# Feed-forward weights, bias rows and first norms prepared inside the second cross attention, with its turns written out on four engines

## The chip, the cores and the metric

The kernel runs on one core of a Trainium2 chip. The core has five instruction streams, and each works through its own in order: PE (TensorE, matrix products and transposes), DVE (VectorE), ACT (ScalarE, functions), POOL (GpSimd) and SP (SyncE, which here only starts DMA transfers). They meet at semaphores. The metric is the device time in microseconds (us).

## The reference

Two batches of 512 tokens of width 512 (x) pass through two layers of a gated cross attention and a gated feed-forward each. The change lies where the last two of these four parts meet:

```python
# second cross attention: 16 heads of 32, keys 1008 + 16 of ctx_1024, q and k normed by head
x = x + tanh(g_xattn[1]) * _L1_xattn_ref(_layernorm(x), ctx_1024, ...)
# second feed-forward
def _act_quant(x):
    scale = 127.0 / clip(max(abs(x), axis=-1, keepdims=True), EPS)
    return clip(round(x * scale), -128.0, 127.0) / scale
def _weight_quant(w):                       # one scale for the whole matrix
    scale = 1.0 / clip(mean(abs(w)), EPS)
    return clip(round(w * scale), -1.0, 1.0) / scale
def _bitlinear(x, w, b):
    return einsum('bsd,hd->bsh', _act_quant(x), _weight_quant(w)) + b
h = gelu(_bitlinear(x, w1, b1))             # w1: 2048 x 512
x = x + tanh(g_ffn[1]) * _bitlinear(h, w2, b2)   # w2: 512 x 2048
```

So both weight matrices (4 MB each in f32) need the mean of their magnitudes before any element can be rounded to -1, 0 or 1. They depend on no activation.

## The kernel before

**The second cross attention** (cross_attention_1). After a front part that makes the queries, the scores are worked off in 8 turns: 4 groups of 4 heads (g) times 2 batches (b). A turn has 16 slots (n): 4 heads by 4 tiles of 128 queries. In slot n

- PE makes the 128 x 1024 scores of n (L2646), transposes the probabilities of slot n-3 (L2607) and in odd slots multiplies transposed probabilities by values (L2624); in slots 5 to 8 it also projects the outputs of the turn before (L2636);
- DVE takes the maximum of the scores of n (L2536, L2537), inverts the sums of n-1 (L2521), makes the low part of the transposed probabilities of n-3 (L2529) and in slots 5 to 8 adds a projected tile to x (L2546);
- ACT copies the high part of n-3 (L2558) and takes the exponentials of n (L2572);
- POOL multiplies the probabilities of n-1 by the inverted sums (L2592), which PE transposes two slots later.

`turns` (L2504) writes the first and the last turn out and puts the six between them into a loop of three iterations of two turns, on PE, DVE, ACT and POOL. SP has a loop of its own over groups: after the last scores of a turn it loads queries and keys of the next group, then its values, and after the turn's x is done the next rows of the output weights (L2319). What follows the last turn (the part "after") has no scores: the last transposes, the last values, and four projections, one behind the other because each waits until DVE has emptied the same bank.

**The feed-forward** (bit_ffn) starts when x is complete (x2_done). Its first matrix is loaded during the attention (raw[0]), the second when x is complete. `sizes` on ACT sums the magnitudes of each with one instruction of 128 x 8192 (L2829); PE sums over partitions with a matrix of ones; DVE makes mean and inverse (L2740, L2742) and scales and rounds 8 chunks of 128 x 2048 with two instructions each (L2748, L2750), ACT makes the third step and the bf16 copy (L2836). Then PE turns both matrices, 16 groups of 8 transposes (L2912), through four banks that ACT (even groups) and DVE (odd groups) empty. Only then do the tiles start: for each of 8 tiles of 128 tokens a norm with rounding on DVE (`norm`), its rounding and transposing (`norm_round`, `norm_turn`, `norm_turned`), the hidden layer on PE (`hidden`), gelu on ACT, `hidden_scale` on DVE, `hidden_round` on ACT, `hidden_turn` and `output` on PE, `add_out` on DVE. The norms run AHEAD = 3 tiles in front.

## Time and profile before

| | us |
|---|---|
| time, median of 3 runs | 2809.32 (2807.34 to 2811.43) |
| the profiled execution, its time | 2806.77 |
| its span in the trace | 2804.9 |

| of the span | busy us | share |
|---|---|---|
| PE | 2392.8 | 85% |
| DVE | 1716.1 | 61% |
| ACT | 1485.5 | 53% |
| POOL | 1096.4 | 39% |

The profiled execution is 1.9 us longer than its span, and 2.6 us below the median of the three runs. The turns of the second cross attention begin at about 2202 us; x is complete at 2642.95; the span ends at 2804.9. Everything before 2202 is the same program in both kernels. Engine shares are means over parts that differ; the rows below are from single stretches. "issue" in a row means that the trace shows nothing that the engine waited for.

### The profile page before, as it was taken

How to read it: one execution, taken by the hardware profiler on the slowest of the kernel's cores; microseconds unless marked ns; L12 is line 12 of the kernel's file. 1: busy time of each engine (PE TensorE's matmuls, PEld its weight loads, DVE VectorE, ACT ScalarE, POOL GpSimd, SP SyncE). 2: the span in 40 equal slices, each digit the busy share in tenths (PEclk: the TensorE clock that was granted, in tenths of full speed). 3: DMA queues.
4: the chain of work that ended last, by engine and by line, in shares of the span. 5: the costliest groups of instructions: out<-in, count | busy, mean ns of one | idle time of the engine just before them, and what ended most of it. 6: DMA issues, size and time to landing. Idle time of an engine off the chain costs nothing. (4 is left out here: it accounts for less than half of the span.)

```text
span 2804.9 us, 46131 instructions
## 1 busy us (share of the span) xinstructions
PE 2392.8 (85%) x14822; PEld 1987.3 (71%) x14830; DVE 1716.1 (61%) x3849; ACT 1485.5 (53%) x3054; POOL 1096.4 (39%) x1553
## 2 busy tenths in 40 slices
PE   5999999999984899898998474999995688989558
PEld 3778878787874788888887353999994576767434
DVE  2555555555554666666666663566655587878576
ACT  3444444444443666656665453444442686777565
POOL 0222232322231444444444265777772654444200
PEclk9999999999997899999999796999997899999869
DMA  3000000000001000000000465677665433233100
GB/s 113 20 12 12 14 19 11 7 19 11 7 1 41 20 1 19 19 19 19 19 19 1 164 207 187 184 202 190 192 177 137 128 91 88 64 74 107 64 1 30
DMA packets 123517, 189.90 MB, mean 68 GB/s; under 512 B 18260, under 2 KB 66644, under 8 KB 121748
## 3 DMA queue, kind: packets, MB, share of 16 engines
q1 hardware_dynamic: 111272, 160.67, 18.9%
q0 software_dynamic: 10992, 25.96, 4.3%
q10 hardware_dynamic: 1152, 2.10, 0.3%
q8 instruction: 42, 0.69, 0.1%
q14 instruction: 59, 0.48, 0.1%
HBM read 142.55 MB, written 46.14 MB: 67 GB/s over the span
## 5 line engine op out<-in xcount | busy, mean ns | idle before, releaser
L435 ACT ACTIVATE x_p<-x_p,x_least 128x1024 f32<-128x1024 f32 x128 | 147.3, 1151 | 307.2 <-DVE x_least L391 307.1
L469 POOL TENSOR_TENSOR x_carry<-x_rtotal 128x1 f32<-128x1 f32 x128 | 24.7, 193 | 559.8 <-DVE x_rtotal L368 559.8
L375 DVE TENSOR_TENSOR x_pT<-pair,x_pT 128x512 fp32r<-128x512 f32 x256 | 164.2, 683 | 122.6 <-ACT x_pT L454 122.6
L2159 PE MATMUL pair<-m_h,e_w 128*128 128x320 f32 x1536 | 230.4, 311 | 1.1 <-DVE m_h L2074 1.1
L2159 PEld LDWEIGHTS pair<-m_h,e_w 128*128 128x128 f32 x1536 | 228.9, 189 | 2.7 <-issue 1.5
L537 PE MATMUL pair<-x_pT,x_v 128*128 128x256 f32 x1536 | 209.6, 293 | 9.2 <-DVE x_pT L375 9.2
L537 PEld LDWEIGHTS pair<-x_pT,x_v 128*128 128x128 f32 x1536 | 194.0, 194 | 26.3 <-issue 18.3
L993 ACT ACTIVATE s_p<-s_p,s_least 128x128 f32<-128x128 f32 (+3 forms) x256 | 143.7, 561 | 123.1 <-DVE s_least L903 123.0
L565 PE MATMUL pair<-x_kT,x_qT 128*128 128x512 f32 x768 | 206.9, 404 | 0.0
L2536 DVE TENSOR_REDUCE z_most<-pair 128x1 f32<-128x1008 f32 x128 | 153.8, 1202 | 82.4 <-PE pair L2646 50.0
L1131 PE MATMUL pair<-s_pT,s_v 128*128 128x256 f32 (+1 forms) x1152 | 158.4, 284 | 47.2 <-DVE s_pT L880 47.2
L1131 PEld LDWEIGHTS pair<-s_pT,s_v 128*128 128x128 f32 x1152 | 152.8, 195 | 59.9 <-issue 30.9
L2558 ACT ACTIVATE z_pT<-pair 128x512 fp32r<-128x512 f32 x256 | 141.7, 601 | 96.2 <-PE pair L2607 81.5
L2607 PE MATMUL pair<-ident,z_p 128*128 128x128 f32 x1024 | 144.8, 281 | 50.8 <-DVE z_pT L2529 49.6
L1053 POOL TENSOR_TENSOR s_carry<-s_rtotal 128x1 f32<-128x1 f32 x256 | 49.7, 194 | 346.6 <-DVE s_rtotal L874 346.3
L2572 ACT ACTIVATE z_p<-pair,z_most 128x1008 f32<-128x1008 f32 (+1 forms) x256 | 174.3, 696 | 14.4 <-DVE z_most L2537 14.4
L2607 PEld LDWEIGHTS pair<-ident,z_p 128*128 128x128 f32 x1024 | 117.4, 143 | 90.4 <-DVE z_pT L2529 62.1
L2592 POOL TENSOR_SCALAR z_p<-z_p,z_rtotal 128x1008 f32<-128x1008 f32 (+1 forms) x256 | 174.5, 694 | 0.0
L880 DVE TENSOR_TENSOR s_pT<-pair,s_pT 128x128 fp32r<-128x128 f32 (+3 forms) x256 | 124.5, 487 | 81.3 <-ACT s_pT L979 81.2
L2529 DVE TENSOR_TENSOR z_pT<-pair,z_pT 128x512 fp32r<-128x512 f32 x256 | 162.7, 676 | 4.6 <-ACT z_pT L2558 3.8
L1808 POOL TENSOR_TENSOR e_w<-e_raw,e_w 128x2048 fp32r<-128x2048 f32 x32 | 146.7, 4588 | 40.2 <-ACT e_w L1774 40.2
L454 ACT ACTIVATE x_pT<-pair 128x512 fp32r<-128x512 f32 x256 | 138.3, 594 | 45.1 <-PE pair L523 45.1
(345 smaller groups left out, 6102.2 us busy)
## 6 DMA issues: line engine op xcount, KB each, us to landing
e_raw<-in_L_ffn_w SPq DMA_DIRECT2D x48, 1024.0 KB, 5.7
z_v<-z_vst SPq DMA_DIRECT2D x16, 768.0 KB, 3.6
z_kS<-z_k SPq DMA_DIRECT2D x24, 512.0 KB, 9.9
z_vS<-z_v SPq DMA_DIRECT2D x8, 1536.0 KB, 7.0
f_raw<-in_L_ffn_w SPq DMA_DIRECT2D x2, 4096.0 KB, 13.4
z_qS<-z_q SPq DMA_DIRECT2D x24, 256.0 KB, 4.4
s_wraw<-in_L_ffn_wq SPq DMA_DIRECT2D x9, 512.0 KB, 4.4
x_wq<-in_L_xattn_Wq SPq DMA_DIRECT2D x8, 512.0 KB, 3.6
```

Source lines behind the costliest of these rows:

```text
L375: dve.tensor_tensor(pT[1][:, keys, q * P:(q + 1) * P], TR[j][:, :].rearrange("p (k n) -> p k n", n=P), pT[0][:, keys, q * P:(q + 1) * P].b ...
L435: act.activation(p[n][:, :], p[n][:, :], ACT.Exp, scale=-1.0, bias=least[:, n:n + 1], accum_out=total[:, n:n + 1]).then_inc(s_ex, 1)
L537: mm = pe.matmul(OB[:, cols], v[x0][b][:, k, :], pT[x1][:, k, cols], start=(half == 0 and n == 0 and k == 0), stop=(half == 1 and n == 2 a ...
L565: mm = pe.matmul(SC[n % 2][:, j * BANK:(j + 1) * BANK], qT[x0][b][n // QT][:, n % QT * P:(n % QT + 1) * P], kT[x1][b][:, j * BANK:(j + 1) ...
L1131: mm = pe.matmul(OB[:, cols], v[b][:, k, first:first + 2, :].rearrange("p k d -> p (k d)"), pT[x1][:, k, cols], start=(i % 2 == 0 and half ...
L1808: pool.tensor_tensor(dst[1][:, :, :], raw[parity][:, :, :], dst[0][:, :, :].bitcast(F32), ALU.subtract).then_inc(s_lo, 1)
L2159: mm = pe.matmul(GU[m % 2][:, j * BANK:j * BANK + CAP], w[x0][:, c, m * P:(m + 1) * P], XS[s][x1][:, c, :], start=(n == 0 and c == 0), sto ...
L2529: dve.tensor_tensor(pT[1][:, k, cols], TR[i][:, :].rearrange("p (k n) -> p k n", n=P), pT[0][:, k, cols].bitcast(F32), ALU.subtract).then_ ...
L2536: dve.tensor_reduce(most[:, w, 0:1], SC[n % 2][:, 0:MAIN], AX.X, ALU.max, negate=True)
L2572: act.activation(p[w][:, cols], SC[n % 2][:, cols], ACT.Exp, bias=most[:, w, k:k + 1], accum_out=total[:, w, k:k + 1]).then_inc(s_ex, 1)
L2592: pool.tensor_scalar(p[w][:, cols], p[w][:, cols], rtotal[:, w, k:k + 1], 1.0, ALU.mult, ALU.mult).then_inc(s_pn, 1)
L2607: mm = pe.transpose(TR[i][:, k * P:(k + 1) * P], p[n % RING][:, kk * P:(kk + 1) * P], ident[:, :])
```

## The change

Three things are done.

1. `every_turn` takes the place of `turns` on DVE, ACT and POOL, and SP's loop over groups becomes a Python loop: all 8 turns are written out on these four engines. PE keeps `turns`, that is, its loop.
2. The weights are made during the turns. A slot is now counted from 0 to 127 over all turns. SP loads both matrices in 8 chunks of 1 MB through two ring buffers, twice. In the first pass ACT sums the magnitudes of chunk i behind slot 4i+3 (`magnitudes`, slots 3 to 31). The sums go to DRAM and come back to every partition (`loads`, turn 2), and DVE adds them up ahead of slot 42 (`means`), in place of the ones matrix. In the second pass POOL rounds chunk i with three instructions, behind slots 48+8i+1, +3 and +5 (`weights`), and behind slots 113, 115 and 117 makes the bias rows and the bf16 identity.
3. The feed-forward is entered differently. Statistics of the first four tiles are taken by DVE ahead of slot 12 of the last turn, their square root by ACT and the norms 0 and 1 by DVE in the part "after". After x2_done PE turns only the 8 groups of the first matrix; those of the second are put between the first tiles' work, through two banks.

The diff, cut to its core:

```diff
@@ back_sync: the loop over groups written out, with the loads
             def back_sync(sp):
-                with sp.Fori(0, NG - 1) as j:
+                sp.wait_ge(s_pj, PJ0 + KVO + NT)
+                for j in range(NG - 1):
                     for b in range(B):
+                        ffn["loads"](sp, B * j + b)
                         sp.wait_ge(s_sc, SC0 + NU * (B * j + b + 1))
...
+                for h in range(B * (NG - 1), TURNS):
+                    ffn["loads"](sp, h)
@@ turns
+            def every_turn(engine, body):
+                for h in range(TURNS):
+                    body(h // B, h % B, "first" if h == 0 else "last" if h == TURNS - 1 else "")
                 body(NG, 0, "after")
@@ back_vector, in slot n of turn h
+                        if own and h * NU + n == MEAN_AT:
+                            ffn["means"](dve)
+                        if part == "last" and n == NU - 4:
+                            ffn["statistics"](dve, 0)
+                        if part == "after" and n == 4:
+                            ffn["first norms"](dve)
...
-                turns(dve, body)
+                every_turn(dve, body)
@@ back_scalar, behind the exponentials of slot n
+                        if own:
+                            ffn["magnitudes"](act, h * NU + n)
+                        if part == "after" and n == LAG:
+                            ffn["root"](act, 0)
@@ back_gpsimd, behind the slot's products
+                        ffn["weights"](pool, h * NU + n)
@@ bit_ffn
+            def loads(sp, turn):
+                if turn == 0:
+                    load(sp, 0)
+                    load(sp, 1)
+                    for i in range(2, 5):
+                        sp.wait_ge(s_red, i - 1)
+                        load(sp, i)
...
+                elif turn == 2:
+                    sp.wait_ge(s_red, CHUNKS)
+                    for w in range(2):
+                        sp.dma_start(sizes[w], size[:, w, :]).then_inc(s_sum, 16)
+                    load(sp, 1)
+                    sp.wait_ge(s_sum, 32)
+                    sp.dma_start(ring[0][:, 0:2 * P * CH], sizes.rearrange("w p k -> (w p k)").partition_broadcast(P)).then_inc(s_sum, 16)
+                    sp.wait_ge(s_mean, 2)
+                    load(sp, 0)
+                elif turn < 7:
+                    for i in {3: (2, 3), 4: (4,), 5: (5, 6), 6: (7,)}[turn]:
+                        sp.wait_ge(s_wq, i - 1)
+                        load(sp, i)
...
+            def means(dve):
+                dve.wait_ge(s_sum, 48)
+                for w in range(2):
+                    dve.tensor_reduce(total[:, w:w + 1], ring[0][:, w * P * CH:(w + 1) * P * CH], AX.X, ALU.add).then_inc(s_mean, 1)
...
+            def magnitudes(act, slot):
+                if slot < SIZED + 4 * CHUNKS and slot % 4 == 3:
+                    i = (slot - SIZED) // 4
+                    act.wait_ge(s_w[i % 2], 16 * (i // 2 + 1))
+                    act.activation(ring[i % 2][:, :], ring[i % 2][:, :], ACT.Abs,
+                                   accum_out=size[:, i // CH, i % CH:i % CH + 1]).then_inc(s_red, 1)
+            def weights(pool, slot):
+                if ROUNDED <= slot < ROUNDED + 8 * CHUNKS:
+                    i, part = (slot - ROUNDED) // 8, slot % 8
+                    w, r = i // CH, ring[i % 2][:, :]
+                    if part == 1:
+                        pool.wait_ge(s_w[i % 2], 16 * (CH + i // 2 + 1))
+                        pool.wait_ge(s_mean, 4)
+                        pool.tensor_scalar(r, r, winv[:, w:w + 1], 1.0, ALU.mult, ALU.min).then_inc(s_wr, 1)
+                    elif part == 3:
+                        pool.wait_ge(s_wr, 2 * i + 1)
+                        pool.tensor_scalar(r, r, -1.0, MAGIC, ALU.max, ALU.add).then_inc(s_wr, 1)
+                    elif part == 5:
...
+                        pool.tensor_scalar(dst, r, -MAGIC, 1.0, ALU.add, ALU.mult).then_inc(s_wq, 1)
...
-            def sizes(act):
-                act.wait_ge(*x2_done)
-                for w in range(2):
-                    act.wait_ge(s_w[w], 16)
-                    act.activation(wq[w][:, :, :], raw[w][:, :, :], ACT.Abs, accum_out=size[:, w:w + 1]).then_inc(s_size, 1)
@@ tensor(pe), after the turns
+                for g in range(GROUPS):
+                    weight_turn(g)
...
                 norm_turn(0)
-                hidden(0)
+                for g in range(GROUPS, GROUPS + 4):
+                    weight_turn(g)
+                    if g == GROUPS + 1:
+                        hidden(0)
                 norm_turn(1)
+                for g in range(GROUPS + 4, 2 * GROUPS):
+                    weight_turn(g)
                 hidden(1)
```

What stands where on three engines:

ACT in the first turn, slots 2 to 4, before (z_p are probabilities, z_pT their transposes):

```order
L2572 ACTIVATE z_p,z_total<-pair,z_most 128x1008
L2572 ACTIVATE z_p,z_total<-pair,z_most 128x16
L2558 ACTIVATE z_pT<-pair 128x4x128 x2
L2572 ACTIVATE z_p,z_total<-pair,z_most 128x1008
L2572 ACTIVATE z_p,z_total<-pair,z_most 128x16
L2558 ACTIVATE z_pT<-pair 128x4x128 x2
```

and in the changed kernel (f_ring is the ring buffer, f_size the sums):

```order
L2591 ACTIVATE z_p,z_total<-pair,z_most 128x1008
L2591 ACTIVATE z_p,z_total<-pair,z_most 128x16
L2577 ACTIVATE z_pT<-pair 128x4x128 x2
L2591 ACTIVATE z_p,z_total<-pair,z_most 128x1008
L2591 ACTIVATE z_p,z_total<-pair,z_most 128x16
L2803 ACTIVATE f_ring,f_size<-f_ring 128x2048
L2577 ACTIVATE z_pT<-pair 128x4x128 x2
```

The sum over chunk 0 stands between slot 3's exponentials and slot 4's copy, and so does each of the seven others.

DVE ahead of slot 42 in the changed kernel, from the end of slot 40 on; before, the three f_ rows weren't there:

```order
L2565 SCALAR_TENSOR_TENSOR x<-pair,tgate,x 128x512
L2555 TENSOR_REDUCE z_most<-pair 128x1
L2556 TENSOR_REDUCE z_most<-pair 128x1
L2534 RECIPROCAL z_rtotal<-z_total 128x2
L2542 TENSOR_TENSOR z_pT<-pair,z_pT 128x4x128 x2
L2792 TENSOR_REDUCE f_total<-f_ring 128x1 x2
L2794 TENSOR_SCALAR f_wmean<-f_total 128x2
L2796 RECIPROCAL f_winv<-f_wmean 128x2
L2555 TENSOR_REDUCE z_most<-pair 128x1
```

Between the tile added to x in slot 8 of turn 2 and the sums over f_ring there is one slot of DVE's work.

PE from the last projections to the first hidden layer, before (L2900 is the ones matrix, L2912 the weights' transposes, L2922 and L2924 a norm's, L2935 and L2937 the hidden layer):

```order
L2636 MATMUL pair<-z_wo,z_oT 128x512 x8
L2900 MATMUL pair<-f_size,f_ones 128x2
L2912 MATMUL pair<-f_identb,f_wq 128x128 x128
L2922 MATMUL pair<-ident,f_u 4x128
L2924 MATMUL pair<-f_identb,f_hq 128x128 x4
L2935 MATMUL pair<-f_brows,f_uT 128x512
```

and in the changed kernel (f_wq_last is a quarter of the second matrix):

```order
L2660 MATMUL pair<-z_wo,z_oT 128x512 x8
L3025 MATMUL pair<-f_identb,f_wq 128x128 x64
L3041 MATMUL pair<-ident,f_u 4x128
L3043 MATMUL pair<-f_identb,f_hq 128x128 x4
L3025 MATMUL pair<-f_identb,f_wq 128x128 x3
L3025 MATMUL pair<-f_identb,f_wq_last 128x128
```

The last two rows stand four times before the first hidden layer (L3054). So of 128 transposes 64 and two further groups of 8 stand ahead of it now; the other six groups stand between it and the second.

## Rows read from the trace of the kernel before

**Rows 1.** Windows of two turns each: us, busy by engine, PE clock, DMA share, GB/s

```profile
2252.90:2353.00 100.10, 91.42 (x611) 73.19 (x610) 86.23 (x169) 79.05 (x198) 48.99 (x97) 1.00 0.35 86
2353.00:2462.20 109.20, 92.69 (x611) 74.66 (x610) 86.33 (x168) 79.24 (x197) 48.92 (x97) 0.97 0.30 76
```

**Rows 2.** Timeline at a loop's end: start, us, engine, line, operation, [idle before <-releaser]

```profile
2352.98 0.63 PE L2646 MATMUL pair<-z_kS,z_qS 96*128 96x512 f32 x2
...
2361.47 1.21 DVE L2536 TENSOR_REDUCE z_most<-pair 128x1 f32<-128x1008 f32 x1 [8.48 <-issue]
```

**Rows 3.** DMA queues in the window 2353 to 2571: packets, MB, share

```profile
q8 instruction: 1, 0.02, 0.0%
```

**Rows 4.** Timeline of an undisturbed pair of slots

```profile
2230.47 0.63 PE L2646 MATMUL pair<-z_kS,z_qS 96*128 96x512 f32 x2
...
2231.14 1.21 DVE L2536 TENSOR_REDUCE z_most<-pair 128x1 f32<-128x1008 f32 x1 [0.66 <-PE pair L2646]
2231.58 1.08 ACT L2558 ACTIVATE z_pT<-pair 128x512 fp32r<-128x512 f32 x2 [0.86 <-PE pair L2607]
...
2233.23 1.16 PE L2607 MATMUL pair<-ident,z_p 128*128 128x128 f32 x8 [0.79 <-DVE z_pT L2529]
```

**Rows 5.** Timeline of the first turn, where slot 3's exponentials end

```profile
2219.20 1.30 SPq L2307 DMA_DIRECT2D z_qS<-z_q  x3
...
2220.44 1.09 ACT L2558 ACTIVATE z_pT<-pair 128x512 fp32r<-128x512 f32 x2
```

**Rows 6.** DMA issues of the span: KB each, us from issue to landing

```profile
e_raw<-in_L_ffn_w SPq DMA_DIRECT2D x48, 1024.0 KB, 5.7
...
z_tbo<-in_L_xattn_bo SPq DMA_DIRECT2D x1, 256.0 KB, 6.5
```

**Rows 7.** Instructions on the tile f_raw: ns min/median/max, first and last start

```profile
L2836 ACT ACTIVATE f_wq<-f_raw x8: 1892/1910/1912, 2668.9 to 2686.1; 128x2048 bf16<-128x2048 f32 x8
```

**Rows 8.** Timeline of the third turn (slots 8 to 11)

```profile
2333.18 0.75 DVE L2546 SCALAR_TENSOR_TENSOR x<-pair,tgate,x 128x512 f32<-128x512 f32 x1
...
2334.11 4.32 SPq L2319 DMA_DIRECT2D z_wo<-in_L_xattn_Wo  x8
...
2336.82 1.21 DVE L2536 TENSOR_REDUCE z_most<-pair 128x1 f32<-128x1008 f32 x1 [0.43 <-PE pair L2646]
...
2340.71 0.19 POOL L2590 TENSOR_TENSOR z_carry<-z_rtotal 128x1 f32<-128x1 f32 x1 [0.92 <-DVE z_rtotal L2521]
```

**Rows 9.** Instructions of POOL by form: busy us, mean ns, idle before

```profile
L1808 POOL TENSOR_TENSOR e_w<-e_raw,e_w 128x2048 fp32r<-128x2048 f32 x32 | 146.7, 4588 | 40.2 <-ACT e_w L1774 40.2
...
L2592 POOL TENSOR_SCALAR z_p<-z_p,z_rtotal 128x1008 f32<-128x1008 f32 x128 | 142.1, 1110 | 0.0
```

**Rows 10.** Instructions on the tile stats: ns min/median/max, first and last start

```profile
L91 DVE BATCH_NORM_STATS2 stats<-x x24: 675/676/695, 9.1 to 2647.2; 128x6 f32<-128x512 f32 x24
```

**Rows 11.** Timeline from the last projections into the feed-forward

```profile
2633.72 0.75 DVE L2546 SCALAR_TENSOR_TENSOR x<-pair,tgate,x 128x512 f32<-128x512 f32 x1 [4.87 <-PE pair L2636]
...
2642.20 0.75 DVE L2546 SCALAR_TENSOR_TENSOR x<-pair,tgate,x 128x512 f32<-128x512 f32 x1 [2.08 <-PE pair L2636]
...
2697.82 0.54 DVE L2781 TENSOR_SCALAR f_h<-x,mv,rstd 128x512 f32<-128x512 f32 x1
...
2700.86 0.54 DVE L2781 TENSOR_SCALAR f_h<-x,mv,rstd 128x512 f32<-128x512 f32 x1
...
2703.38 0.79 PE L2935 MATMUL pair<-f_brows,f_uT 4*128 4x512 f32 x1 [0.83 <-ACT f_hqT L2857]
...
2714.83 0.18 PEld L2935 LDWEIGHTS pair<-f_brows,f_uT 4*128 4x128 f32 x1 [3.50 <-issue]
...
2724.75 2.29 DVE L2769 TENSOR_REDUCE f_most<-f_z 128x1 f32<-128x2048 f32 x1 [1.53 <-ACT f_z L2863]
```

**Rows 12.** Instructions of ACT from 2643 to 2725 by line: busy us, mean ns

```profile
L2822 ACT ACTIVATE f_w1T<-pair 128x1024 bf16<-128x1024 bf16 x4 | 4.0, 1016 | 1.0 <-PE pair L2912 1.0
...
L2849 ACT ACTIVATE f_hq<-f_h 128x512 bf16<-128x512 f32 x3 | 1.9, 630 | 3.9 <-DVE f_h L2786 3.9
```

More of the change, by code:

```diff
@@ L2695, in bit_ffn @@
             uT = [sb(f"f_uT{s}", [4, P], F32R) for s in range(2)]
-            with ExitStack() as early:
-                braw = early.enter_context(nc.sbuf_tensor("f_braw", [2, HID], F32))
-                blow = early.enter_context(nc.sbuf_tensor("f_blow", [2, HID], F32R))
-            z = [sb(f"f_z{s}", [P, HID]) for s in range(2)]
             zq = [sb(f"f_zq{s}", [P, HID], BF16) for s in range(2)]
@@ L2707, in bit_ffn @@
             TRZ = [banks[6 + i][:, :].bitcast(BF16) for i in range(2)]
-            WTB = [pairs[2 + i // 2][:, (i % 2) * BANK:(i % 2 + 1) * BANK].bitcast(BF16) for i in range(4)]
+            WTB = [banks[k][:, :].bitcast(BF16) for k in (6, 7, 4, 5)]
             s_w = [sem("f_w1"), sem("f_w2")]
-            s_b, s_size, s_sum, s_mean, s_wr, s_wq, s_wt, s_wa, s_wd = [
-                sem(f"f_{n}") for n in ("b", "size", "sum", "mean", "wr", "wq", "wt", "wa", "wd")]
+            s_b, s_red, s_sum, s_mean, s_wr, s_wq, s_wt, s_wa, s_wd = [
+                sem(f"f_{n}") for n in ("b", "red", "sum", "mean", "wr", "wq", "wt", "wa", "wd")]
@@ new lines, in half_statistics, with half_root @@
+            def half_statistics(dve, k):
+                tiles = range(k * QT, (k + 1) * QT)
+                dve.wait_ge(*(half_done, x2_done)[k])
+                for t in tiles:
+                    dve.bn_stats(stats[:, 6 * t:6 * t + 6], x3[:, t, :]).then_inc(s_stat, 1)
+                for t in tiles:
+                    dve.wait_ge(s_stat, 3 * NT + t + 1)
+                    dve.bn_aggr(mv[:, 2 * t:2 * t + 2], stats[:, 6 * t:6 * t + 6]).then_inc(s_mv, 1)
+            def half_root(act, k):
+                act.wait_ge(s_mv, 3 * NT + (k + 1) * QT)
+                act.activation(std[:, k * QT:(k + 1) * QT], mv[:, :].rearrange("p (t k) -> p t k", k=2)[:, k * QT:(k + 1) * QT, 1], ACT.Sqrt,
+                               bias=eps[:, 0:1]).then_inc(s_std, 1)
@@ L2721, in sync, with half_inverse @@
+            def half_inverse(dve, k):
+                dve.wait_ge(s_std, 4 + k + 1)
+                dve.reciprocal(rstd[:, k * QT:(k + 1) * QT], std[:, k * QT:(k + 1) * QT]).then_inc(s_rstd, 1)
+                dve.wait_ge(s_rstd, 4 + k + 1)
+            ffn["loads"], ffn["means"], ffn["weights"] = loads, means, weights
+            ffn["magnitudes"] = magnitudes
+            ffn["statistics"], ffn["root"] = half_statistics, half_root
             def sync(sp):
-                sp.wait_ge(*x1_read)
@@ L2754, in vector, with first_norms @@
+            def first_norms(dve):
+                half_inverse(dve, 0)
+                for t in range(2):
+                    norm(dve, t)
+            ffn["first norms"] = first_norms
+            def vector(dve):
+                for g in range(1, GROUPS, 2):
                     dve.wait_ge(s_wt, g + 1)
                     turned(dve, g)
-                dve.wait_ge(s_rstd, 5)
-                steps = 0
-                def step(ins):
-                    nonlocal steps
-                    steps += 1
-                    ins.then_inc(s_ch, 1)
-                    dve.wait_ge(s_ch, steps)
@@ L2881, in scalar @@
                 norm_round(0)
+                norm_round(1)
+                half_root(act, 1)
                 norm_turned(0)
-                norm_round(1)
-                norm_turned(1)
-                gelu(0)
+                for g in range(GROUPS, 2 * GROUPS, 2):
+                    act.wait_ge(s_wt, g + 1)
+                    turned(act, g)
+                    if g == GROUPS + 2:
+                        norm_turned(1)
+                        gelu(0)
                 norm_round(2)
@@ L2974, in tensor @@
                         norm_turn(t + AHEAD)
-            programs["ACT"].append(sizes)
-            statistics(3, x2_done, 1)
             programs["SP"].append(sync)
```

197 lines of the change are left out of this document (112 added, 85 removed).

## The prediction

> **What bounds the kernel now.** I read the stages first, then the chain, then the single waits. The stages: two turns without a loop's end take 100.1 us, the same 611 matrix instructions with one take 109.2 [rows 1], and the second such window, 2462 to 2571, repeats that. At the loop's end PE has already begun the next turn's scores at 2352.98, DVE comes back at 2361.47 after 8.48 us of "issue", that is, with nothing to wait for [rows 2]. Inside a turn PE and DVE hold each other: scores, DVE's maximum, DVE's low part, PE's transposes, values, and back; DVE idles 0.66 us and ACT 0.86 us in a pair of slots of 5.6 us [rows 4]. (In 100.1 us DVE is busy 86.2 and ACT 79.1 [rows 1]; most of the idle time lies in the slots with projections.) So whatever is put on DVE or ACT in an ordinary slot must fit into less than 1 us. After the turns, x is complete at 2642.20 + 0.75 = 2642.95 (T below), the first norm starts at 2697.82, the first hidden layer at 2703.38, the second at 2714.83 and DVE meets the second gelu at 2724.75 [rows 11]. From there on one tile follows the other at an even pace that the change leaves alone. Hence T to T+81.8 is the stretch to recompute.
>
> **What goes: the feed-forward's entry.** In the changed order, counted from T: PE's first 8 transposes about 0.5; ACT empties four banks at 1.02 [rows 12], T+4.5, while DVE empties the odd four. ACT then rounds two norms at 0.63 [rows 12], T+5.8. DVE takes statistics of the other four tiles, 4 x 0.68 [rows 10] with a little for the means, T+7.1; ACT's square root waits for that, and then come the small evictions (0.83 us of PE's waiting before [rows 11]): first hidden layer at T+8.4, where it was at T+60.4. It takes 7.8 us, as before in my reading of the trace from 2703.38 on; two groups of w2 and a norm's transposes bring PE to about T+17.7. ACT: eviction of that norm, table load and gelu to T+22.0, one eviction of w2 to T+23.0, and only then can PE fill that bank again and finish w2: second hidden layer at T+24.0 instead of T+71.9 [rows 11]. What follows is as before. **Gain 48 us.** The first layer alone would say 52; the interleaved w2 groups give 4 back, since the bank is waited for behind gelu. With all of PE's pieces at the half clock it is 45.
>
> **What goes: the loop's ends.** Two of them at 109.2 - 100.1 = 9.1 [rows 1], **18.2 us**; a third pass ends by falling through and shows no gap. What is late next is PE's own loop, which stays. Between 2353 and 2571, two further passes, the instruction queue 8 moves one packet [rows 3], and PE's scores at 2352.98 came without a gap, so PE has its loop at hand and I count its branch at nothing. The Trainium skill, "Runtime: NRT & Kernel Launch", section on instruction fetch mechanics, says that prefetch is purely sequential and a taken branch to a target outside the current two pages forces a fetch; it also gives PE four times the buffer. DVE's 8.48 us agree with the first half; taken to the letter for PE too, the rule would leave the stall where it is and make this term 0. The queue's row speaks for 18.2.
>
> **What comes: ACT's eight sums.** One is 1.91 us for 2048 columns [rows 7] with 0.19 to read the sum, 2.1. It stands ahead of the copy of the next slot. ACT idles 0.86 there, DVE may start 0.3 after the copy's first half, so some 1.0 is exposed; seven times, one of them in a projection slot where PE is behind anyway: **6 us** (0 to 14).
>
> **The first sum waits for its data.** SP's last loads for the front start at 2219.20 and take 1.3 to issue, and only behind them comes chunk 0, about 2220.7. ACT is through with slot 3 and goes on with the next copy at 2220.44 [rows 5], where it now waits. A 1 MB load lands 5.7 after its issue [rows 6]; here 768 KB go ahead of it and a second chunk beside it, so I take 7.5. With the sum itself and some slow clock after the pause, **10 us** (6 to 14). Behind the waiting ACT are the copies that DVE and then PE need, so all stand.
>
> **DVE ahead of slot 42 waits for the sums' round trip.** SP can only send them after its eight loads of output weights, which start at 2334.11 when x's last tile of the turn before is done and take 3.75 to 4.3 [rows 8]. Then two stores and chunk 1 (1.2), the stores' landing (about 1.9, from my reading of the 64 KB loads), and the broadcast of 512 KB behind 1 MB of chunk 1. The nearest row is the last of three loads, 1.5 MB in all, that lands 6.5 after its own issue [rows 6]. Issue at about 2341, landing at about 2347. DVE would begin slot 42 at 2336.82 [rows 8]: 10 us of waiting, then two sums over 512 (some 0.7 each) and two small operations, 1.9; with PE's clock down for a while after such a pause **13 us** (8 to 18). Behind DVE's wait the maximum of slot 42 is queued, for which ACT and PE wait.
>
> **POOL's 24 roundings.** A tensor_scalar of 1008 columns takes 1.11 [rows 9], so 2048 take about 2.0 to 2.2 (the dearest two-tensor form 4.59 [rows 9], which bounds it above; I take the nearer form). Eight slots cost POOL 12.4, three roundings 6.3, of 22.4: it fits, and a result is used two slots later. Two places don't fit. Chunk 7 is issued behind the output weights of turn 6, so it lands about 2334.1 + 3.8 + 0.4 + 5.7 = 2344 on turn 2's scale, while POOL is through with its slot at about 2339.8 and has the next one due at 2340.71 [rows 8]; with the rounding this makes that slot 5.5 late, of which some 2.2 are slack: **3 us**. The bias row's difference in slot 115 (4.6 by the two-tensor row, on two partitions) **1 us**.
>
> **DVE's early statistics and norms.** Four statistics in slot 12 of the last turn: 2.8, less DVE's idle 0.66: **2.3 us**. Norms 0 and 1 cost 2700.86 - 2697.82 = 3.04 each, 6.3 with the inverse; DVE idled 4.87 before the first projection [rows 11], and ACT's table load and root hold the norms back by 0.8: **2.3 us**.
>
> **Sum.** 48 + 18.2 = 66.2 off; 6 + 10 + 13 + 3 + 1 + 2.3 + 2.3 = 37.6 on; net 28.6. The profiled execution took 2806.8, so 2778.2; it stood 2.6 below the median of the runs, and on the median's scale it is 2780.7. I say 2780.
>
> **The rivals.**
> - *The two waits are short.* Speaks for it: the DMA engines are idle from 2224 on, and a lone 1 MB load is quick; against it: SP's order, which fixes the issue. With both at half my price it is 2780 - 10 = 2770; with ACT's sums hidden as well, 2765.
> - *The fetch stall stays*, at PE's branch, or because straight code on DVE and ACT runs into the 12 MB of further loads in the turns. For it: the rule above, and that both ends of loop fell into a burst of loads; against it: [rows 3], and turns 0 and 7, straight code under loads, show no gap. 2780 + 18 = 2798.
> - *Everything added is exposed*: ACT's sums at 2.1, POOL's roundings pushing one slot in each chunk by 1. 2780 + 8 + 8 = 2796.
> - *Slower than before: POOL's roundings run at the two-tensor rate.* One mechanism: two slots with a rounding need 3.1 + 4.6 = 7.7 against 5.6. In each chunk the first rounding then costs 1.1 (4.6 less 1.3 of gap, less 2.2 of slack), the next two 2.1 each; 5.3 a chunk, 42 in all: 2780 + 42 = 2822. It decides from about 4.1 us for one rounding. For it: all rows of two-tensor form on POOL; against it: 128 rows of the very form at 1.11.
>
> **How the numbers follow.** Forecast 0.56 (2770 to 2790), short waits 0.14, stall stays 0.11, all exposed 0.12, POOL slow 0.05, and 0.02 for nothing of this. 0.2% (about 5.6 us) is what a measurement can tell from no change. The range 2764 to 2799 takes in the first four. Faster takes all four cases but their edges, 0.91; slower is POOL's case and a rest, 0.05; same 0.04.
>
> **What would show it.** In the profile after: no 8 us of "issue" on DVE and ACT in the turns, and two turns without additions at 100.1; a wait of ACT of some 7 us for f_ring in the first turn, and one of DVE of some 10 in the third; POOL's roundings near 2.1; one wait of POOL for chunk 7 in the seventh turn; the first hidden layer 8 to 9 us and the second about 24 us after x is complete. The prediction is wrong if a gap of 8 us appears on PE at its branch, if a rounding takes over 3 us, or if the entry gives less than 45.

## The result, and the profile after

The changed kernel takes **2843.35 us** (median of 4 runs, 2838.82 to 2848.59) against 2809.26 for the kernel before in the same comparison: ratio 1.012, 95% interval 1.0108 to 1.0132. It is 34 us slower; 2780 had been forecast. The profiled execution took 2838.82, its span is 2837.0. Each experiment below was measured beside the kernel before in a comparison of its own, in which that kernel's median lies between 2809 and 2817 us; between comparisons the ratios count, not the medians.

The table cuts the spans at the same instructions: the front's last load of queries (where the row of turn 0 begins), then the first load of queries after each turn's last scores, and the end of x's last tile (T). "No clamp" is the first experiment below. In the forecast the 6 us of ACT's seven other sums are spread evenly, three to turn 0 and four to turn 1.

| stretch, us | before | after | no clamp | forecast for after |
|---|---|---|---|---|
| turn 0 | 30.2 | 42.7 | 43.8 | 42.8 |
| turn 1 | 50.2 | 54.3 | 52.6 | 53.6 |
| turn 2 | 49.9 | 63.9 | 65.7 | 62.9 |
| turns 3 and 4 | 109.2 | 126.5 | 100.2 | 100.1 |
| turn 5 | 59.2 | 64.7 | 50.1 | 50.1 |
| turns 6, 7 and the rest, to T | 125.0 | 151.7 | 135.6 | 133.6 |
| T to the end | 162.0 | 114.1 | 115.6 | 114.0 |
| together | 585.7 | 618.0 | 563.5 | 557.1 |

The feed-forward's entry gave what was forecast. The timeline of the kernel after, from x's last tile (which ends at T = 2722.92) to DVE's meeting with the second gelu (start, duration, engine, line, instruction, idle time before it and what ended it), answers to [rows 11]:

```profile
2722.17 0.75 DVE L2565 SCALAR_TENSOR_TENSOR x<-pair,tgate,x 128x512 f32<-128x512 f32 x1 [2.08 <-PE pair L2660]
...
2731.20 0.50 PE L3054 MATMUL pair<-f_brows,f_uT 4*128 4x512 f32 x1 [1.68 <-ACT f_hqT L2969]
...
2746.77 0.79 PE L3054 MATMUL pair<-f_brows,f_uT 4*128 4x512 f32 x1
...
2756.81 2.29 DVE L2877 TENSOR_REDUCE f_most<-f_z 128x1 f32<-128x2048 f32 x1 [1.64 <-ACT f_z L2975]
```

First hidden layer 8.3 us behind T (forecast 8.4), second 23.9 (24.0), DVE at the second gelu 33.9 where it was 81.8: 47.9 gained of 48.

The time went in the turns from slot 48 on, where POOL rounds. POOL's three roundings of each chunk, by form (busy us, mean ns), stand against [rows 9]:

```profile
L2814 POOL TENSOR_SCALAR f_ring<-f_ring,f_winv 128x2048 f32<-128x2048 f32 x8 | 57.3, 7166 | 2.9 <-DMA f_ring<-in_L_ffn_w 2.9
...
L2817 POOL TENSOR_SCALAR f_ring<-f_ring 128x2048 f32<-128x2048 f32 x8 | 56.7, 7091 | 0.0
...
L2823 POOL TENSOR_SCALAR f_wq<-f_ring 128x2048 bf16<-128x2048 f32 x7 | 13.3, 1899 | 0.0
```

Two of three take 7.1 us, 3.5 ns a column, where the 1.11 us of [rows 9] for 1008 columns had let 2.0 to 2.2 be expected. What that does to the others, in the timeline of the fourth turn:

```profile
2391.52 1.36 POOL L2615 TENSOR_SCALAR z_p<-z_p,z_rtotal 128x1008 f32<-128x1008 f32 x2
...
2392.86 7.16 POOL L2814 TENSOR_SCALAR f_ring<-f_ring,f_winv 128x2048 f32<-128x2048 f32 x1
...
2400.17 1.35 POOL L2615 TENSOR_SCALAR z_p<-z_p,z_rtotal 128x1008 f32<-128x1008 f32 x2
...
2401.65 1.97 PE L2631 MATMUL pair<-ident,z_p 128*128 128x128 f32 x8 [4.84 <-POOL z_p L2615]
...
2402.99 7.09 POOL L2817 TENSOR_SCALAR f_ring<-f_ring 128x2048 f32<-128x2048 f32 x1
```

POOL does its own products of slot 49 (z_p), then the 7.16 us, and only then the products of slot 50, for which PE has been waiting 4.84 us. Those of slot 51 and the second long instruction follow. Behind the wait PE's eight transposes take 1.97 us; those of an ordinary slot take 1.04 to 1.25 in this trace, so the pause costs clock as well. PE's wait stands in the list of waits (us in total, times, longest), together with the three that the change was expected to bring:

```profile
PE pair L2631 <- POOL z_p L2615: 53.8, 12, 7.7
...
DVE f_total L2792 <- DMA f_ring<-f_sizes: 10.4, 1, 10.4
...
ACT f_ring L2803 <- DMA f_ring<-in_L_ffn_w: 7.2, 1, 7.2
...
POOL f_ring L2814 <- DMA f_ring<-in_L_ffn_w: 2.9, 1, 2.9
```

Before, PE waited 1.1 us for z_p over the same stretch. The two turns that answer to the undisturbed pair of [rows 1], with POOL busy 108 us instead of 49 and PE's granted clock at 0.89 (columns as there):

```profile
2380.01:2506.52 126.51, 99.37 (x608) 80.64 (x608) 86.75 (x170) 79.80 (x197) 108.13 (x104) 0.89 0.33 91
```

### The profile page after: what moved, and what is told of

The parts are those of the page before. It is cut to its first block and busy times, and to the rows that moved or that the text cites. A ratio compares the mean times of both kernels' runs of the same rounds, so it can differ in the third digit from the quotient of the medians.

```text
span 2837.0 us, 45204 instructions
## 1 busy us (share of the span) xinstructions
PE 2411.6 (85%) x14828; PEld 2002.3 (71%) x14828; DVE 1698.1 (60%) x3834; ACT 1470.8 (52%) x3057; POOL 1230.3 (43%) x1580
## 5 line engine op out<-in xcount | busy, mean ns | idle before, releaser
L2631 PE MATMUL pair<-ident,z_p 128*128 128x128 f32 x1024 | 152.2, 293 | 107.6 <-POOL z_p L2615 54.8
L2631 PEld LDWEIGHTS pair<-ident,z_p 128*128 128x128 f32 x1024 | 125.2, 150 | 145.1 <-issue 82.2
```

What stands on the lines that cost most here:

```text
L2631: mm = pe.transpose(TR[i][:, k * P:(k + 1) * P], p[n % RING][:, kk * P:(kk + 1) * P], ident[:, :])
```

## The experiments

### What the roundings cost, and why

**The clamps left out (e1).** The two long instructions keep shape, types, place and waits; only an operation of each is another.

```diff
-pool.tensor_scalar(r, r, winv[:, w:w + 1], 1.0, ALU.mult, ALU.min)
+pool.tensor_scalar(r, r, winv[:, w:w + 1], 1.0, ALU.mult, ALU.mult)
-pool.tensor_scalar(r, r, -1.0, MAGIC, ALU.max, ALU.add)
+pool.tensor_scalar(r, r, 1.0, MAGIC, ALU.mult, ALU.add)
```

> The changed kernel with POOL's two clamps left out: (multiply, min 1) becomes (multiply, multiply by 1), and (max -1, add) becomes (multiply by 1, add); shapes, types, waits and number of instructions stay, and the weights' codes are no longer limited to -1..1. Theory A, the arithmetic function decides: both forms fall from 7.1 us to about 1.9, PE's waits for POOL's z_p fall from 54 us to under 5, x is complete some 60 us earlier, and the kernel takes 2775 to 2790. Theory B, a 2048-column f32 result written over its own source is slow on POOL, or DVE's and the loads' traffic slows it: both forms stay at 7.1 us and the time at 2839 to 2848. Theory C, POOL's instructions matter but another of the added waits takes their place: the forms fall to 1.9, and the time stays above 2800.

Measured: 2784.83 us (2784.14 to 2787.61), ratio to before 0.9902 (0.9886 to 0.9919). POOL by form:

```profile
L2814 POOL TENSOR_SCALAR f_ring<-f_ring,f_winv 128x2048 f32<-128x2048 f32 x8 | 16.0, 1999 | 2.8 <-DMA f_ring<-in_L_ffn_w 2.8
L2817 POOL TENSOR_SCALAR f_ring<-f_ring 128x2048 f32<-128x2048 f32 x8 | 15.3, 1910 | 0.0
```

Theory A holds; B and C are out. From turn 3 to T the run is 57.1 us shorter than the changed kernel (285.9 against 342.9), and turns 3 and 4 now take, in the window that answers to [rows 1], as long as the pair without a loop's end (100.15 and 100.10 us):

```profile
2384.39:2484.54 100.15, 91.43 (x608) 73.25 (x608) 86.19 (x170) 79.04 (x197) 69.69 (x107) 1.00 0.43 116
```

Of the 57.1 us, 43.0 are more idle time of PE. The other 14.1 are PE's same instructions taking longer (264.5 us busy against 250.4), at a granted clock of 0.88 to 0.93 in the rows from turn 3 to T, against 0.96 to 1.00 here.

**One clamp left out at a time (e2, e3).** The first pair of lines of this diff alone, and the second alone.

> The changed kernel with only (multiply, min 1) replaced by (multiply, multiply by 1); (max -1, add) stays (the codes have no upper limit). Theory A: the first form falls to 1.9 us and the second stays at 7.1; each of the 16 long instructions costs about as much of the end as another, so half of the loss comes back: 2805 to 2815. Theory B: nothing changes, 2839 to 2848. If one long instruction in a chunk fits into POOL's slack, nearly all comes back: below 2795.

> The changed kernel with only (max -1, add) replaced by (multiply by 1, add); (multiply, min 1) stays (the codes have no lower limit). Theory A: the second form falls to 1.9 us, the first stays at 7.1, 2805 to 2815, as with the other half left out. Theory B: 2839 to 2848. If only min were slow and not max: the second form at 7.1 with this edit would fall by nothing, and the run without min would have given all.

Measured: without (multiply, min) 2817.8 us, ratio 1.0023 (1.0013 to 1.0032); without (max, add) 2831.5, ratio 1.0068 (1.0052 to 1.0085). B is out again: the form whose clamp is left out falls to 2.0 and 1.9 us and the other stays at 7.1 and 7.2. But both times miss A's 2805 to 2815, and with them its even split: the first instruction of a chunk alone costs 43 us from turn 3 to T (328.9 against 285.9), the second alone 31. The timelines of PE show why. With only the first one long (e3), PE waits 4.83 to 4.85 us in each of the first seven chunks, and 8.13 us in the last:

```profile
2402.52 1.96 PE L2631 MATMUL pair<-ident,z_p 128*128 128x128 f32 x8 [4.85 <-POOL z_p L2615]
```

With only the second one long (e2), it waits 4.74 us in every other chunk and 0.8 to 0.9 in the ones between (the last chunk, whose data come late, has 2.5 and 3.7). In the ones between POOL's long instruction (2398.76 to 2405.86 in the first of them) falls into the slots with projections, and PE has two of them (L2660) to do meanwhile:

```profile
2399.30 1.98 PE L2660 MATMUL pair<-z_wo,z_oT 128*128 128x512 f32 x4 [0.22 <-ACT z_oT L2582]
...
2404.35 1.88 PE L2660 MATMUL pair<-z_wo,z_oT 128*128 128x512 f32 x4
...
2407.50 1.09 PE L2631 MATMUL pair<-ident,z_p 128*128 128x128 f32 x8 [0.81 <-POOL z_p L2615]
...
2436.11 1.96 PE L2631 MATMUL pair<-ident,z_p 128*128 128x128 f32 x8 [4.74 <-POOL z_p L2615]
```

That the projections are what fills the wait is read from this timeline; no run moved them. The waits of e3 add up to 7 x 4.84 + 8.13 = 42 us, but that they nearly equal its 43 is chance: PE's idle time grew by 34 us, and 9 are its slower instructions. Together the two long instructions cost 57, less than the sum of 74: behind the first one's wait the second finds PE later than it would otherwise, and in the changed kernel its waits of 4.74 are 2.6 to 3.0, those of 0.8 are gone, and only in chunk 7 it is 3.9.

**POOL's instructions alone (e0).** The changed kernel, and behind its end:

```diff
...
+                pool.wait_ge(s_x2, NT)
...
+                done(pool.memset(r1, 0.3))          # done: and wait for it
...
+                for _ in range(2):
+                    done(pool.tensor_scalar(r0, r1, one, 1.0, ALU.mult, ALU.min))
...
+                    done(pool.tensor_scalar(r0, r1, 1.0, -1.0, ALU.min, ALU.max))
...
```

> The changed kernel, and behind its last result 26 instructions of POOL alone, one after the other, with DVE, ACT, PE and the DMA queues idle (its total time is of no interest). Theory A, the function decides: over 2048 f32 columns every form with min or max takes about 7.1 us, also with another tile as target, with one operation only, and with a bf16 result; multiply with multiply, and multiply with add, take 1.9; time goes with the columns (1024: 3.6, 256: 0.9). Theory B, company on the memory's ports: alone, the forms with min or max take 1.9 to 4 as the others do. Theory C, two clamps in one instruction (min, max) cost twice one. Open, and of use for a repair: whether a comparison (is_gt) costs as little as a multiplication.

The timeline; in order (multiply, min), (multiply, multiply), (max, add), (multiply, add), min, max, (min, max), (multiply, is_gt); then (multiply, min) into bf16 and, last, a product of two tensors (left out: (multiply, min) 3.71 over 1024 columns and 1.14 over 256, a copy 1.89):

```profile
2844.58 7.16 POOL L3118 TENSOR_SCALAR f_ring<-f_ring,f_winv 128x2048 f32<-128x2048 f32 x1
2851.84 1.98 POOL L3119 TENSOR_SCALAR f_ring<-f_ring,f_winv 128x2048 f32<-128x2048 f32 x1
2853.90 7.09 POOL L3120 TENSOR_SCALAR f_ring<-f_ring 128x2048 f32<-128x2048 f32 x1
2861.08 1.90 POOL L3121 TENSOR_SCALAR f_ring<-f_ring 128x2048 f32<-128x2048 f32 x1
2863.06 5.37 POOL L3122 TENSOR_SCALAR f_ring<-f_ring 128x2048 f32<-128x2048 f32 x1
2868.51 5.36 POOL L3123 TENSOR_SCALAR f_ring<-f_ring 128x2048 f32<-128x2048 f32 x1
2873.95 1.89 POOL L3124 TENSOR_SCALAR f_ring<-f_ring 128x2048 f32<-128x2048 f32 x1
2875.95 7.17 POOL L3125 TENSOR_SCALAR f_ring<-f_ring,f_winv 128x2048 f32<-128x2048 f32 x1
...
2888.24 7.15 POOL L3128 TENSOR_SCALAR f_wq<-f_ring,f_winv 128x2048 bf16<-128x2048 f32 x1
...
2897.43 4.49 POOL L3130 TENSOR_TENSOR f_ring<-f_ring 128x2048 f32<-128x2048 f32 x1
```

B is out: alone, over a constant 0.3 and into another tile, the forms take the same 7.1 as among the turns. But A as I had put it is wrong as well, and so is C. (min, max) takes **1.89 us**, less than either alone (5.37). So it is not the function but the pair.

**More pairs, and DVE (e4).** The same frame with other pairs, and four of them on DVE behind POOL's.

> As the first run of instructions of POOL alone behind the changed kernel's end, with 15 other pairs of operations on 2048 f32 columns, and four of them on DVE. Theory P, a pair runs fast only if both operations are of one family (multiply, add, subtract, or min, max): (max, min), (min, min) and the two with a scalar in memory 1.9 us; (multiply, max), (add, min), (max, multiply), (min, multiply) 7.1. Theory Q, only the order (arithmetic first, then compare, or the other way) decides: one of the mixed orders at 1.9. One operation alone with no second: multiply and add at 1.9 if the missing second counts as nothing, at 5.4 as min and max alone did if the missing second is what is slow. On DVE all four forms take 1.2 to 2.3 us, the pairing plays no part.

(multiply, max); multiply alone; (add, add); (min, min); (max, min); (subtract, multiply); (min, max) with the first scalar from memory; then on DVE two instructions at a time, of which the first two are (multiply, min) and (multiply, multiply):

```profile
2849.64 7.16 POOL L3118 TENSOR_SCALAR f_ring<-f_ring,f_winv 128x2048 f32<-128x2048 f32 x1
2856.89 5.45 POOL L3119 TENSOR_SCALAR f_ring<-f_ring,f_winv 128x2048 f32<-128x2048 f32 x1
...
2869.60 7.11 POOL L3121 TENSOR_SCALAR f_ring<-f_ring 128x2048 f32<-128x2048 f32 x1
...
2883.96 7.08 POOL L3123 TENSOR_SCALAR f_ring<-f_ring 128x2048 f32<-128x2048 f32 x1
2891.12 7.08 POOL L3124 TENSOR_SCALAR f_ring<-f_ring 128x2048 f32<-128x2048 f32 x1
...
2918.07 7.10 POOL L3128 TENSOR_SCALAR f_ring<-f_ring 128x2048 f32<-128x2048 f32 x1
...
2937.89 1.97 POOL L3131 TENSOR_SCALAR f_ring<-f_ring,f_winv 128x2048 f32<-128x2048 f32 x1
...
2941.01 2.61 DVE L3140 TENSOR_SCALAR f_ring<-f_ring,f_winv 128x2048 f32<-128x2048 f32 x2 [95.25 <-POOL f_ring L3132]
```

Theories P and Q both fall. Of all the pairs tried four run at 0.93 to 0.97 ns a column: (multiply, multiply), (multiply, add), (min, max) and, in the kernels' third rounding, (add, multiply). The twelve others, (add, add), (subtract, multiply), (max, min) and (min, min) as well as every mixed one, take 3.5 ns; one operation with no second takes 2.6, even a multiplication, though a copy takes 0.92. What sets the four apart the traces do not show; they show only the times. On DVE the pairing plays no part: the first two instructions take 2.61 us together, (max, add) and (min, max) together 2.49, and each of the four 1.2 to 1.3. The Trainium skill, "GPSIMD Engine Reference", section 4.1 Engine selection, calls work with one input on this engine roughly line-rate. Of 16 pairs and 5 single operations here only the four pairs come near one column a nanosecond, and so does the copy (1.89 us). The Trainium skill, "GPSIMD Engine Reference", section 3.1, gives 4497 ns for a two-tensor addition of this size, and the product in the last row of the first list agrees with 4.49 us.

**The same three steps, paired for speed (f1).** Rounding comes before clamping, so that the clamp is a (min, max) against the constant plus and minus 1; the codes are complete.

```diff
-pool.tensor_scalar(r, r, winv[:, w:w + 1], 1.0, ALU.mult, ALU.min)
+pool.tensor_scalar(r, r, winv[:, w:w + 1], MAGIC, ALU.mult, ALU.add)
-pool.tensor_scalar(r, r, -1.0, MAGIC, ALU.max, ALU.add)
+pool.tensor_scalar(r, r, MAGIC + 1.0, MAGIC - 1.0, ALU.min, ALU.max)
```

> The changed kernel with the same three instructions a chunk on POOL, paired differently: (multiply by 1/mean, add the rounding constant), then (min, max) against the constant plus and minus 1, then as before; the clamp is complete. The instructions alone took 1.9 us for (multiply, add) and for (min, max), against 7.1 for (multiply, min) and (max, add). If the pairing is what decides: all three at 1.9 to 2.0 us among the turns too, and the time of the run without clamps, 2783 to 2788. If min and max are slow only with the other engines at work: the second stays above 5 us and the time is 2810 to 2820, as in the run with one long instruction a chunk.

Measured: 2787.9 us (2787.2 to 2795.1), ratio 0.9910 (0.9896 to 0.9925), that of the run without clamps within the intervals. The first instruction takes 1.99 us, and the (min, max) among the turns what it took alone:

```profile
L2817 POOL TENSOR_SCALAR f_ring<-f_ring 128x2048 f32<-128x2048 f32 x8 | 15.2, 1897 | 0.7
```

Two lines turn 1.2% slower into 0.9% faster.

### The loop's ends

The kernel before, with `every_turn` on DVE, ACT and POOL and nothing else (u1).

```diff
-                turns(dve, body)
+                every_turn(dve, body)      # and so on ACT and POOL
```

> The kernel before with one part of the change alone: the turns written out on DVE, ACT and POOL (SP and PE keep their loops, and the feed-forward is as before). My reading: the two gaps of 8 us of issue at the loop's ends go, turns 3 and 5 fall from 59.2 us to 50, and the time is 18.2 lower, 2791 to 2794. Rival, the fetch stall stays on PE's branch or comes back as gaps in straight code: the time stays within 5 us of before, and the gaps stand on PE or are scattered. Rival, SP's or PE's own loop was half of it: 9 lower, 2802.

Measured: 2795.7 us against 2815.75 in the same comparison, ratio 0.9927 (0.9914 to 0.9939): 20 us less, 18.2 forecast. Inside the traces, from the front's last load of queries to T, it is 405.7 us against 423.8, 18.1 less. SP's loads behind each turn's last scores:

```profile
2356.24 1.33 SPq L2307 DMA_DIRECT2D z_qS<-z_q  x3
...
2406.37 1.29 SPq L2307 DMA_DIRECT2D z_qS<-z_q  x3
...
2456.30 1.32 SPq L2307 DMA_DIRECT2D z_qS<-z_q  x3
```

These turns are 50 us apart, as are the others; the rivals are out. PE keeps its loop, and no gap stands at its branch. In the window 2353 to 2571 the queue "q14 instruction" moved 21 packets in the kernel before and moves 8 in this run, so the gaps went together with packets of instructions. The queue q8, from which the prediction took that PE has its loop at hand, moves one packet in both; which engine a queue serves the profile does not say.

### The two waits

**ACT's sums three slots later (f2).** On f1:

```diff
-            SIZED, ROUNDED = 0, 48
+            SIZED, ROUNDED = 3, 48
-                if slot < SIZED + 4 * CHUNKS and slot % 4 == 3:
+                if SIZED <= slot < SIZED + 4 * CHUNKS and (slot - SIZED) % 4 == 3:
```

> The run before this one, and ACT's eight sums each three slots later (slots 6, 10 to 34 in place of 3, 7 to 31). In the profile ACT waited 8.4 us for the first chunk; three slots are 8.4 us. My theory: that wait goes with some slow clock behind it, 8 to 11 us less, 2773 to 2778. Rival, the pause moves: chunk 0's landing is not what is late, or the last sum, now at slot 34, holds the sending of the sums and lengthens DVE's wait at slot 42 by as much: no gain, 2784 to 2788.

**The sums sent ahead of the output weights (f3).** On f1:

```diff
+                    if j == 0:
+                        ffn["sent"](sp)      # stores, load(1), broadcast: was in loads, turn 2
                     sp.wait_ge(s_wd, WD0 + QT * (B * j + B))
                     load_out(sp, j + 1)
```

> The run f1, and SP sends the sums (two stores, chunk 1's load, the broadcast) ahead of the eight loads of output weights instead of behind them; ACT's sums stay where they were. DVE waited 11.6 us for the broadcast at slot 42. My theory: the sums are there by slot 36, the wait goes with the slow clock behind it, 11 to 15 us less, 2770 to 2775. Rival, the output weights come later and PE's projections wait for them: half or none of it, 2778 to 2786.

In the run f1 that both start from, the waits are:

```profile
DVE f_total L2792 <- DMA f_ring<-f_sizes: 10.4, 1, 10.4
...
ACT f_ring L2803 <- DMA f_ring<-in_L_ffn_w: 7.9, 1, 7.9
```

Later sums: 2779.7 us, ratio 0.9868 (0.9853 to 0.9882) against 0.9910, 12 us by the ratios and 8 by the medians; ACT's wait is gone from the list, DVE's is 11.3. The wait goes, as my theory has it, but the time stays 2 us above its range: turns 0 and 1 take 10.9 us less, and turn 2, which begins earlier and still waits for the sums, 2.6 more (66.4 against 63.8). Sent early: DVE's wait is gone, turn 2 takes 53.2 us instead of 63.8, but the median is 2786.4 (2768.8 to 2791.2), ratio 0.9883 (0.986 to 0.9907), and my range of 2770 to 2775 is missed. The rival's reason is not it: no wait of PE for the output weights stands in the list. The profile has 10.7 us more behind turn 5 than f1 (258.2 against 247.5), with DVE's, ACT's and POOL's busy time the same and PE's 11.0 us longer for the same work; its granted clock is lower. Half of it lies in the last three projections, which take 3.78 us each here and 1.98 each in f1, behind gaps of the same length (3.04, 0.84 and 0.84). One execution of six kept the gain, and no profile of it was taken.

**All together (f4)**, with chunk 7's load ahead of the output weights as well:

```diff
+                    elif j == 2:
+                        ffn["seventh"](sp)   # wait_ge(s_wq, 6), load(7): was in loads, turn 6
```

> The run f1 (clamps paired as min with max) with both edits tried singly (ACT's sums three slots later, the sums sent ahead of the output weights) and a third: the load of chunk 7 ahead of the output weights of its turn, for which POOL waited 2.8 us. If each wait goes and none takes its place, the end of the turns comes 8 + 11 + 3 = 22 us earlier than in f1, and the time is 2762 to 2768. In f3 the turns were 11 us shorter and the whole only 2 in its profile (in one execution 19), because TensorE ran at half clock in more of the stretch from the last projections into the feed-forward (granted clock 0.70 and 0.76 there against 0.89 and 0.70). If that clock falls by chance from one execution to the next, the times here spread over some 15 us, 2762 to 2780; if an early end of the turns itself brings it, all executions stand near 2775.

Measured: 2765.8 us (2760.1 to 2771.0), ratio 0.9836 (0.9821 to 0.9852). It lies in the range of the first statement, and none of the three waits stands in the list any more. The spread of 11 us, with no execution near 2775, speaks for chance and not for an early end.

### The clock at the entry

The timeline of PE in f4: the second and third projection of the last turn, then the start of the first hidden layer.

```profile
2637.60 3.38 PE L2664 MATMUL pair<-z_wo,z_oT 128*128 128x512 f32 x4 [3.11 <-DVE x L2569]
2641.83 1.98 PE L2664 MATMUL pair<-z_wo,z_oT 128*128 128x512 f32 x4 [0.84 <-DVE x L2569]
...
2655.72 0.50 PE L3064 MATMUL pair<-f_brows,f_uT 4*128 4x512 f32 x1 [1.68 <-ACT f_hqT L2979]
2656.15 1.04 PE L3066 MATMUL pair<-f_w1T,f_hqT 128*128 128x512 bf16 x4
...
2657.54 1.89 PE L3066 MATMUL pair<-f_w1T,f_hqT 128*128 128x512 bf16 x4
```

The same projection takes 3.38 us and then 1.98, and in the hidden layer the same four products 1.04 and, 1.4 us later, 1.89: TensorE falls to 1.2 GHz behind a gap of 3.11 us, and behind gaps of 1.34 and 1.68 that follow each other, and comes back to 2.4. It is not so each time: in f1 the projection behind a gap of 3.04 takes 1.98, in f3 3.78. The granted clock of the stretch behind f4's last projection:

```profile
2647.00:2690.00 43.00, 33.06 (x221) 17.08 (x222) 25.40 (x57) 23.94 (x30) 0.00 (x0) 0.84 0.02 7
```

**The gaps filled with idle transposes (f5)**, up to T; on f4, with 6 more behind the last projection:

```diff
+                            if part == "after":
+                                fill(pe, 20 if t == 1 else 6)   # transposes of ident into TR[0]
                             pe.wait_ge(s_wd, WD0 + QT * (h - 1) + t)
```

> The run before this one, and 44 idle transposes of the identity on PE (results unused) in the gaps in which PE waits for DVE to add a tile of x: 20 before the second of the last four projections, 6 before the third and fourth, 6 before the weights' transposes. At full clock they fit into the gaps (0.84 to 3.04 us) to within 0.3 each. My theory: PE's pauses there are what lets the clock fall to its lower level, where a projection takes 3.8 us instead of 2.0 and the first hidden layer 9 instead of 5; with the pauses filled the clock stays at 1.00 to the end of the first hidden layer, and the time is 5 to 12 below the run before, and spreads less. Rival: the clock falls for another reason, the fillers only delay: 0 to 5 slower.

(The kernel has 38 of them, 20 + 6 + 6 + 6, and the trace shows as many; the 44 is a slip.) Measured: 2761.5 us (2755.2 to 2768.9), ratio 0.9816 (0.9802 to 0.9829). All four projections take 1.98, but the hidden layer is still at 1.89; the profile is that of the slowest execution. The intervals of f4 and f5 overlap: the gain of 4 us is not shown, and the executions spread by 14 us, not less than f4's 11.

**And on behind T (f6)**, 61 more, on f5:

```diff
+                idle(9)                      # transposes of ident into the output's bank
                 norm_turn(0)
...
+                        idle(11)
                         hidden(0)
...
+                    if g == 2 * GROUPS - 2:
+                        idle(28)
                     weight_turn(g)
```

> The run f5, and 61 more idle transposes on PE behind x's completion: 9 before the first norm's transposes, 11 before the first hidden layer, 28 before the last two groups of w2 (where PE waits 3.9 us for ACT), 4 and 9 before the first layer's codes and the third hidden layer. In f5 the projections all ran at full clock (1.98 us each) and the clock fell only behind the gaps of 1.34 and 1.68 us that follow. My theory: it is these gaps; with them filled the first two hidden layers take 1.5 us a block instead of 2.5 in both, 8 to 10 us in all at most, and the ratio to the kernel before falls from 0.9816 to about 0.979. Rival: the clock falls after a time whatever PE does there: the fills only delay, ratio 0.982 to 0.984, and blocks of 2.5 us stay.

Measured: 2760.0 us (2758.6 to 2762.5) against 2816.9, ratio **0.9801** (0.9788 to 0.9814). PE, and the window:

```profile
2639.74 1.98 PE L2672 MATMUL pair<-z_wo,z_oT 128*128 128x512 f32 x4 [0.85 <-DVE x L2569]
...
2655.04 1.37 PE L3102 MATMUL pair<-ident 128*128 128x128 f32 x11
...
2658.19 1.04 PE L3075 MATMUL pair<-f_w1T,f_hqT 128*128 128x512 bf16 x4
```

```profile
2647.00:2690.00 43.00, 38.81 (x322) 25.13 (x323) 27.06 (x59) 25.97 (x33) 0.00 (x0) 1.00 0.02 7
```

The clock is 1.00 where it was 0.84 in f4, every block of the hidden layers in this window takes 1.4 us, and the five executions lie within 4 us instead of 14: in this window the rival is out. Against f4 the intervals do not overlap; against f5's (0.9802 to 0.9829) they do, so beyond f5 the clock and the steadiness are what shows, not the gain. By its ratio this is the fastest version, 2.0% below the kernel before and some 3% below the changed one.

## Why the prediction was wrong

The step that failed is the one on POOL's roundings: "A tensor_scalar of 1008 columns takes 1.11, so 2048 take about 2.0 to 2.2 ... I take the nearer form". The row of [rows 9] was (multiply, multiply), the new instructions (multiply, min) and (max, add), and I read the row by its name and shape and not by its operations. They take 7.1 to 7.2 us. With that, "it fits" is wrong: their roundings, for which the sum has nothing but the 3 us at chunk 7, cost 57 us from turn 3 to T against the same instructions at 1.9 to 2.0. The clamp's third instruction, (add, multiply), came at 1.9.

The rival "POOL's roundings run at the two-tensor rate" had the way of the loss and its place right (POOL's next products come late and PE waits for them), and a chance of 0.05. The rate it names was not the one, for two of three roundings took 3.5 ns a column and the third 0.9; and its threshold of 4.1 us no run tested. Its 4.59 was called an upper bound, which it was not: a bound from another form bounds nothing here. By its own formula, 4.6 replaced by 7.1: 3.6 for a chunk's first, 4.6 for its second, nothing for the third, 66 for eight chunks; 57 came. That this is near is in part luck: the first made PE wait 4.8 in nearly every chunk and not 3.6, the second only in every other chunk, and PE's slower clock has no place in the formula.

The rest stands, measured in the run without clamps, which on the first comparison's scale is 0.9902 x 2809.3 = 2782 against the forecast 2780. (Its profile is that of its slowest execution, and the stretches of the table add up to 563.5 in it, 6.4 above the forecast.)

- *Entry*, 48: 47.9 in the changed kernel; in this run 46.4 to the end, 48.1 up to the second gelu.
- *Loop's ends*, 18.2: 9.1 for turns 3 and 4 together and 9.1 for turn 5. Alone (u1) they gave 20. No gap showed at PE's branch. The rule in the Trainium skill, "Runtime: NRT & Kernel Launch", section on instruction fetch mechanics, taken to the letter for PE too, would have left one there; the trace does not agree.
- *First sum waits*, 10 with 7.5 of waiting: 7.2 waited in the changed kernel, 8.4 in this run. *ACT's other sums*, 6: turn 0, with the wait and three sums, is 13.6 longer, and turn 1, with four, 2.4; 16 for both terms, as forecast.
- *DVE ahead of slot 42*, 13 with 10 of waiting: 10.4 and 11.6 waited, turn 2 is 15.7 longer.
- *Chunk 7, bias row, early statistics and norms*, 8.6: 10.6 in the last stretch. POOL waited 2.8 for chunk 7.

So in this run five of the table's seven stretches were off by 1 to 3 us each, one of them downwards, and one term, put at nothing, was 57. In the rival of the short waits "half my price" of 10 + 13 is 11.5, and not the 10 that was taken off; nothing hangs on it.

## What to carry to other kernels

A row prices an instruction only for its operations. Before work moves to POOL, look for a row with the same pair, and if there is none, take the dearest rate as a guess and not as a bound, or run the one instruction. Where a formula of several steps has freedom, pair its steps so that each instruction is one of the fast pairs; here rounding before clamping was worth 2.1% (ratio 1.012 against 0.991), some 59 us. And behind each gap in PE's work look at the granted clock of what follows: 99 idle transposes in gaps of 1 to 4 us bought 0.35%, some 10 us, and steadier times.

## What was not expected of the hardware

- POOL over 128 x 2048 f32: 1.9 us for (multiply, multiply), (multiply, add), (add, multiply), (min, max); 7.1 for each other pair tried; 5.4 for one operation alone, so that adding a second can make an instruction 2.8 times faster (1.98 against 5.45 for multiply, 1.89 against 5.37 for min). The second operand of the kernel before's products, a multiplication by 1.0, is such a case.
- A bf16 result changes nothing (7.15 us against 7.16), and neither do another target, other values and what the other engines do (7.16 alone, 7.17 in place among the turns).
- What POOL's long instruction costs PE depends on what stands beside it: 4.74 us where PE had no projections to do, 0.8 to 0.9 where it had.
- Executions of one kernel differ by up to 22 us (f3) and the fastest of them had the highest mean granted clock (0.950 against 0.942 to 0.946). Between the profiles of f1 and f3 half of the 10.7 us is in three projections of 3.78 us for 1.98. The two levels of the changed kernel's own runs, 2839 (mean clock 0.940 in both) and 2848 (0.934, 0.937), may be the same; no profile of a run at 2848 shows where.
